# Expert loop of a mixture-of-experts decoder block: the down product one block further behind, waits at matmuls with fixed addresses, four buffers of turned rows

## What is computed

```python
probs = jax.nn.softmax(x @ gate_w, axis=-1)
w, sel = jax.lax.top_k(probs, K)                  # K = 8 of E = 32
w = w / jnp.sum(w, axis=-1, keepdims=True)
...
xg = x_pad[t_slot].reshape(E, C, H)               # the queue of each expert
g = jnp.einsum('ech,ehi->eci', xg, w_gate)        # H = 256, i = 96
u = jnp.einsum('ech,ehi->eci', xg, w_up)
y = jnp.einsum('eci,eih->ech', jax.nn.silu(g) * u, w_down).reshape(E * C, H)
out = jnp.zeros((T + 1, H), x.dtype).at[t_slot].add(w_slot[:, None] * y)
```

## Time and profile before

| | us |
|---|---|
| median of 3 runs | 625.38 |
| lowest and highest run | 624.90, 626.18 |
| span of the profiled execution | 719.4 |
| attention stages in it, up to | 350 |
| PE's expert loop in it | 389.4 to 658.5 |
| PE busy in the span | 563.9 (78%) |
| ACT, DVE, POOL busy | 330.1, 368.4, 390.5 |

### The profile page before, as it was taken

The page is one execution under the profiler, slowest core; times in us unless marked ns, Lnnn a source line. Parts: engine busy times, 40 slices in busy tenths (PEclk is TensorE's granted clock), DMA queues, the critical chain, the costliest instruction groups (busy, mean ns, idle before and its releaser), DMA issues.

```text
span 719.4 us, 17476 instructions
## 1 busy us (share of the span) xinstructions
PE 563.9 (78%) x5097; PEld 414.4 (58%) x5098; DVE 368.4 (51%) x1527; ACT 330.1 (46%) x1204; POOL 390.5 (54%) x599
## 2 busy tenths in 40 slices
PE   3768787888878888888306889988998888985995
PEld 2445454544555554444105777777777776774884
DVE  1537566666677566666402444444444444443453
ACT  2445555455455455456003555555555554553012
POOL 5443445545544455545551666766666666665432
PEclk9789999999999899999556999999999999998899
DMA  9999996111111111112285554555555454554994
GB/s 206 277 275 365 342 339 231 69 59 73 68 50 64 55 73 73 65 66 74 99 308 182 155 165 150 160 156 167 152 164 159 143 157 142 164 160 148 425 418 145
DMA packets 83069, 121.31 MB, mean 169 GB/s; under 512 B 13779, under 2 KB 72669, under 8 KB 80992
## 3 DMA queue, kind: packets, MB, share of 16 engines
q1 hardware_dynamic: 64128, 78.46, 36.3%
q0 software_dynamic: 14016, 38.44, 14.7%
q10 hardware_dynamic: 4896, 4.03, 1.7%
HBM read 56.07 MB, written 69.01 MB: 174 GB/s over the span
## 4 chain that ended last, share of the span: by engine, by line
PE 54%; issue 12%; ACT 12%; DVE 9%; DMA 6%; ACTq 3%; POOL 2%; SPq 1%; another core or an unknown queue 0%; DVEq 0%; POOLq 0%
PE bank L793 14%; PE bank L809 9%; ACT pr L870 7%; PE bank L611 5%; PE bank L785 5%; PE bank L601 4%; PE bank L803 3%; PE bank L661 3%; DMA out<-fin 3%; PE bank L744 2%; DMA wall<-results 2%; DVE nmax L1024 2%; PE bank L619 2%; ACTq L296 1%; DVE tg L1218 1%
## 5 line engine op out<-in xcount | busy, mean ns | idle before, releaser
L556 POOL DMA_INDIRECT results<-ys,wcol x152 | 150.1, 988 | 25.8 <-POOL pscrap L545 22.0
L530 POOL DMA_INDIRECT queues<-x,xidx x128 | 129.1, 1009 | 36.9 <-issue 36.5
L793 PE MATMUL bank<-wall,xtT 128*128 x616 | 127.1, 330 | 0.7 <-issue 0.7
L870 ACT ACTIVATE pr<-bank,nmax 128x128 f32<-128x128 f32 x256 | 90.9, 370 | 29.1 <-DVE nmax L1024 29.1
L1218 DVE SCALAR_TENSOR_TENSOR tg<-th,bank 128x96 f32<-128x96 f32 x154 | 39.1, 254 | 125.3 <-ACT th L957 96.9
L793 PEld LDWEIGHTS bank<-wall,xtT 128*128 128x128 f32 x616 | 98.4, 194 | 1.4 <-issue 1.3
L963 ACT ACTIVATE ys<-bank,wcol 128x256 f32<-128x256 f32 x152 | 71.9, 473 | 54.6 <-PE bank L809 36.6
L809 PE MATMUL bank<-wall,hT 96*128 x304 | 94.5, 392 | 0.0
L785 PE MATMUL bank<-ident,xt 128*128 128x128 f32 x310 | 63.3, 286 | 35.4 <-DMA xt<-queues 24.1
L785 PEld LDWEIGHTS bank<-ident,xt 128*128 128x128 f32 x310 | 59.0, 197 | 49.9 <-DMA xt<-queues 25.1
L876 ACT COPY prT<-bank 128x512 f32<-128x512 f32 x64 | 38.5, 601 | 88.9 <-PE bank L611 86.2
(11 more groups left out here) (178 smaller groups left out, 947.2 us busy)
## 6 DMA issues: line engine op xcount, KB each, us to landing
xt<-queues SPq DMA_DIRECT2D x162, 160.0 KB
results<-zeros SPq DMA_DIRECT2D x16, 1024.0 KB
wall<-results SPq DMA_DIRECT2D x16, 1024.0 KB, 12.7
queues<-zeros SPq DMA_DIRECT2D x32, 160.0 KB, 4.9
wall<-in_L_ffn_w_gate SPq DMA_DIRECT2D x4, 768.0 KB
wall<-in_L_ffn_w_up SPq DMA_DIRECT2D x4, 768.0 KB
wall<-in_L_ffn_w_down SPq DMA_DIRECT2D x4, 768.0 KB
results<-ys,wcol POOLq DMA_INDIRECT x152
```

Of the source, the lines that this page charges most:

```text
L530: pool.indirect_dma_start(xg, bass.IndirectOffsetOnAxis(ap=xidx[:, par, k:k + 1], axis=0), x2[:, par, :], None, bounds_check=last_row, oob ...
L556: pool.indirect_dma_start(yr, bass.IndirectOffsetOnAxis(ap=wcol[:, u, 1:2], axis=0), ys[:, u, :], None, bounds_check=last_y, oob_is_err=Fa ...
L793: ins = pe.matmul(bank[2 + u % 2][:, 0:2 * INTER].rearrange("p (g i) -> p g i", g=2), xtT[:, u % 2, kk, :], wall[:, bass.ds(e, GU)].rearrange(
L870: ins = act.activation(pr[:, g % 2, q, :], pS[g % 2][:, q * P:(q + 1) * P], ACT.Exp, bias=nmax[:, 4 * g + q:4 * g + q + 1], accum_out=den[ ...
```

## The change

The loop's body for block t becomes, on PE, `block_T(t + 4)`, `gu(t + 3)`, `turn_h(t + 2)`, `down(t)`, and on ACT and DVE correspondingly; `weights` stays at t + 2. So the down product comes two blocks behind the turn of its rows, not one, and `hT` has four buffers. The wait for `dveF["hT"]` ahead of `down` is gone, and the semaphore with it: on DVE the copy of block t's `hT` stands ahead of the gate of block t + 2, for which PE's `turn_h(t + 2)`, ahead of `down(t)`, waits. The wait for `actF["xT"]` moves from `gu` to the second transpose of `block_T`, whose address is fixed. Three registers are carried from round to round, and the lead-in has one block more.

```diff
--- before.py
+++ after.py
@@ -30,6 +30,7 @@
 LEAD = UN - 2
+DEEP = 3
 IDLE = 2 * UN + 2
...
         hg = sb("hg", [P, 2, INTER])
-        hT = sb("hT", [INTER, 2, P])
+        hT = sb("hT", [INTER, 4, P])
         wcol = sb("wcol", [P, UN, 2], I32)
...
         actF = {n: sem(f"actF_{n}") for n in ("xT", "th", "y")}
-        dveF = {n: sem(f"dveF_{n}") for n in ("w", "tg", "hg", "hT")}
+        dveF = {n: sem(f"dveF_{n}") for n in ("w", "tg", "hg")}
         drained = sem("drained")
...
@@ -779,16 +780,14 @@
                 s = u % UN
 
                 pe.wait_ge(xt_in[s], 16 * (j + (u // UN + 1)))
-                if isinstance(t, int) and t >= 2:
-                    pe.wait_ge(actF["xT"], t - 1)
-                for kk in range(2):
-                    ins = pe.transpose(bank[u % 2][:, kk * P:(kk + 1) * P],
-                                       xt[:, s, kk:D:2], ident[:, :])
-                ins.then_inc(peF["xT"], 1)
+                pe.transpose(bank[u % 2][:, 0:P], xt[:, s, 0:D:2], ident[:, :])
+
+                if there(t - 1):
+                    pe.wait_ge(actF["xT"], t)
+                pe.transpose(bank[u % 2][:, P:2 * P], xt[:, s, 1:D:2], ident[:, :]).then_inc(peF["xT"], 1)
 
             def gu(t, u, e):
 
-                pe.wait_ge(actF["xT"], t + 1)
                 for kk in range(2):
                     ins = pe.matmul(bank[2 + u % 2][:, 0:2 * INTER].rearrange("p (g i) -> p g i", g=2),
                                     xtT[:, u % 2, kk, :],
@@ -805,28 +804,32 @@
 
             def down(t, u, e):
 
-                pe.wait_ge(dveF["hT"], t + 1)
-                pe.matmul(bank[6 + u % 2][:, 0:D], hT[:, u % 2, :], wall[0:INTER, bass.ds(e, WX)][:, GU:WX],
+                pe.matmul(bank[6 + u % 2][:, 0:D], hT[:, u % 4, :], wall[0:INTER, bass.ds(e, WX)][:, GU:WX],
                           start=True, stop=True).then_inc(peF["y"], 1)
             for t in range(3):
                 block_T(t, t, 0)
-            last_two = [nc.alloc_register(ET.PE, f"last_two{u}") for u in range(2)]
-            carried = [bass.RuntimeValue.of_register_unchecked(r).with_bounds(min_val=0, max_val=(NE - 1) * WX) for r in last_two]
-            for t, e in zip((0, 1), neighbours(ET.PE, tab_g[0:1, LEAD:UN], (NE - 1) * WX)):
-                pe.reg_mov(last_two[t], e)
-                gu(t, t, e)
+            last = [nc.alloc_register(ET.PE, f"last{u}") for u in range(DEEP)]
+            carried = [bass.RuntimeValue.of_register_unchecked(r).with_bounds(min_val=0, max_val=(NE - 1) * WX) for r in last]
+            first = neighbours(ET.PE, tab_g[0:1, LEAD:LEAD + DEEP], (NE - 1) * WX)
+            for t in range(DEEP):
+                pe.reg_mov(last[t], first[t])
+            gu(0, 0, first[0])
+            block_T(3, 3, 0)
+            gu(1, 1, first[1])
             turn_h(0, 0)
+            gu(2, 2, first[2])
+            turn_h(1, 1)
             with pe.Fori(0, rounds) as j:
-                e = neighbours(ET.PE, tab_g[0:1, bass.ds(j * UN + UN, UN)], (NE - 1) * WX)
+                e = neighbours(ET.PE, tab_g[0:1, bass.ds(j * UN + LEAD + DEEP, UN)], (NE - 1) * WX)
                 for u in range(UN):
                     t = j * UN + u
-                    block_T(t + 3, u + 3, j)
-                    gu(t + 2, u, e[u])
-                    turn_h(t + 1, u + 1)
-                    down(t, u, e[u - 2] if u >= 2 else carried[u])
-                for u in range(2):
-                    pe.reg_mov(last_two[u], e[UN - 2 + u])
+                    block_T(t + 4, u + 4, j)
+                    gu(t + 3, u + 3, e[u])
+                    turn_h(t + 2, u + 2)
+                    down(t, u, e[u - DEEP] if u >= DEEP else carried[u])
+                for u in range(DEEP):
+                    pe.reg_mov(last[u], e[UN - DEEP + u])
...
@@ -968,13 +971,15 @@
                 act.copy(spare[0:1, k:k + 1], tab_n[0:1, 0:1]).then_inc(actF["y"], 1)
             for t in range(3):
                 block_T(t, t)
-            for t in range(2):
-                tanh(t, t)
+            tanh(0, 0)
+            block_T(3, 3)
+            tanh(1, 1)
+            tanh(2, 2)
             with act.Fori(0, rounds) as j:
                 for u in range(UN):
                     t = j * UN + u
-                    block_T(t + 3, u + 3)
-                    tanh(t + 2, u)
+                    block_T(t + 4, u + 4)
+                    tanh(t + 3, u + 3)
                     y(t, u)
...
@@ -1224,20 +1229,22 @@
             def h_T(t, u):
 
                 dve.wait_ge(peF["hT"], t + 1)
-                dve.tensor_copy(hT[:, u % 2, :], bank[4 + u % 2][0:INTER, 0:P]).then_inc(dveF["hT"], 1)
+                dve.tensor_copy(hT[:, u % 4, :], bank[4 + u % 2][0:INTER, 0:P])
 
             for t, column in zip((0, 1), neighbours(ET.DVE, tab_w[0:1, 0:UN], D + NE - 1)[LEAD:]):
                 weights(t, t, 0, column)
             for t in range(2):
                 gate(t, t)
             h_T(0, 0)
+            gate(2, 2)
+            h_T(1, 1)
             with dve.Fori(0, rounds) as j:
                 columns = neighbours(ET.DVE, tab_w[0:1, bass.ds(j * UN + UN, UN)], D + NE - 1)
                 for u in range(UN):
                     t = j * UN + u
                     weights(t + 2, u + 2, j, columns[u])
-                    gate(t + 2, u)
-                    h_T(t + 1, u + 1)
+                    gate(t + 3, u + 3)
+                    h_T(t + 2, u + 2)
```

## The result

The changed kernel takes 657.38 us (median of 4 runs, 656.0 to 658.51) against 625.78 us (4 runs, 624.9 to 626.59) for the kernel before: 1.051 times, 95% interval 1.049 to 1.0531. That is 31.6 us slower. The forecast was 624.3 us with a range up to 628.3, so it was wrong by far more than its range.

The account below looks back on a forecast made before the run. The prediction took PE's own pace, 11.4 us a round, plus 0.77 us around each turn as the bound. From 625.38 us, -3.4 at the turns and +2.3 in the lead-in gave 624.3 us, range 616.0 to 628.3.

Parts of the forecast that it names:

- The table load: At the round's turn on PE's sequencer: 557 to 809 ns, not hidden, some 0.5 us of the gap stay.
- The choice on late signals: Loop: L803's 34 waits for hg (27.9 us in 17 rounds) are a cost of being profiled, absent from the runs.
- Rival 1: Loop: the late hg signals are real, so L809's waits go in the runs too: 618.2 us, at most 614; chance 0.15.
- the forecast span of 712 us: Profiled execution: L809's idle 0.16 us behind each of some 38 late hg falls away, -6.1 us more.
- -3.4 us at the turn: Round's turn: without the wait on hT, address work starts at hg's end, 0.19 us earlier at 18 turns.
- The wait that was removed: Down product's wait on hT at the turn: its removal was to bring the 0.19 us.
- +2.3 us of lead-in: Ahead of the loop: one more block and a later first load delay its start by 2.3 us, bounds +1.5 to +3.1.
- The other zeros: Loop: the moved xtT wait, POOL, the block loads and the extra register move were each to cost nothing.
- Rival 2: Round's turn: the sequencer passes a waiting matmul, so the whole turn is hidden, -13.9 us: 613.8 us; chance 0.07.
- Rival 3: Round's first block: DVE's late gate takes back the turn's gain, lead-in stays: 627.7 to 628.5 us; chance 0.17.
- the forecast of -1.1 us: Whole kernel: -3.4 us at the turns and +2.3 us in the lead-in.

Follow-up runs that it names:

- b0_before: The kernel before, unchanged, run again for a second profiled execution: 624.12 us, span 622.5 us.
- a1_aligned: The changed kernel with PE's table of gate offsets written earlier, so each round's load begins at entry 8j + 8: 627.43 us, 1.0035.
- d_mid2: The changed kernel with both table loads, PE's and DVE's, moved to mid-round, from entry 8j + 12: 615.71 us, 0.984.
- a2_wait_back: The changed kernel with loads at 8j + 8 and the wait on hT put back at the down product: 627.48 us, 1.0036.
- b_w1: The kernel before with DVE's table one entry later and its loads at 8j + 9, PE's loads untouched: 640.97 us, 1.0247.
- c_mid2: The kernel before with both table loads, PE's and DVE's, moved to mid-round, from entry 8j + 12: 617.21 us, 0.9859.
- b_shift1: The kernel before with PE's table one entry later and its loads at 8j + 9: 657.36 us, 1.0538.
- b_shift2: The kernel before with PE's table two entries later and its loads at 8j + 10, one run: 657.66 us.

## Why the prediction was wrong, step by step

**The table load: the step that failed.** The prediction took the load's 557 to 809 ns as given, and said of its place at the turn that it "isn't hidden". Both are true of the kernel before. What it didn't price is that the change moves the load's start from 8j + 8 to 8j + 9, though the index stands in the diff. It costs, in the traces, 2.223 - 0.668 us (the means over the turns) x 18 turns = 28.0 us, and 1.948 - 0.601 = 1.35 us for the load of the first round: 29.3 us. Nothing covers the added part, for PE has some 0.35 us of queued matmuls left when the load begins. No bound was set on a load from another start, as there was no row for it in the trace; that absence should have widened the range upward.

**The rest of the 31.6 us.** From the traces of before (span 622.5) and after (655.4): the first transposes of the loop start at 334.31 instead of 328.93 us, 5.4 us later: 1.35 of it is the first slow load, 0.95 that the first block was turned later (323.66 for 322.71), and about 3.1 the longer lead-in. From there to the last turn it is 248.05 instead of 220.43 us: 27.6. Together 33.0 us, and the spans differ by 32.9. Of the 27.6 us, 25.9 are 18 rounds at 13.68 instead of 12.245 us; the other 1.8 are one slow stretch in the first round, behind the slow load (see the last section). A round is only 1.44 us longer, though its load is 1.555: the change gained 0.12 us at each turn, of which the next paragraphs tell.

**The choice on late signals** gave the right number for a wrong reason. They are not in the runs, as the forecast said, and the turn was worth 0.66 + 0.11 us, the round 12.2 us: 12.245 in b0_before. But they aren't the cost of being profiled, for which the prediction took them: the spans of b0_before and of the changed kernel are 1.6 and 2.4 us below their runs. Rival 1 falls with them, and so does the forecast span of 712 us.

**-3.4 us at the turn: the register work moved as forecast, the gain didn't come.** Over the 18 turns of b0_before (medians) the register instruction of L809 starts 0.04 us behind the end of the hT copy and 0.16 us ahead of L803's matmul; in a1_aligned L807's starts 0.05 us behind the end of hg and 0.35 us ahead of L802's matmul. That is 0.19 us earlier, just as the prediction had it. Two things then took it back. The third register move is in one instruction with the others, as forecast, but that instruction takes 103 ns in place of 47, and "nothing" should have been 0.056 us. And the load, which begins 0.115 us earlier, takes 0.752 us in the mean in place of 0.668. With the first block, 0.03 us longer, the round of a1_aligned is 12.236 us long, that of b0_before 12.246: 0.2 us gained in all. The wait of the round's first transposes for issue, forecast to shrink from 16.8 to 13.5 us in 17 rounds, is 16.1 there, for 16.6 in b0_before. Why the load is longer there is open. It isn't simply that matmuls run beside it, for in d_mid2 it lies wholly beside them and takes 0.596 us.

**The wait that was removed** gained nothing by itself (a2_wait_back). The prediction put the 0.19 us down to it. With the wait put back the register work still starts 0.05 us behind hg, so the 0.19 us comes with the extra block of distance.

**+2.3 us of lead-in: within its bounds, at the upper one.** a1_aligned is 2.5 us slower than before. In its trace the loop starts 3.0 us later, 3.1 us counted from the first transposes. Step by step: L792 starts 3.15 us behind the first transposes where L793 started 2.35 us behind them, +0.8 as forecast. The copy of block 2 ends at 327.85, near where the forecast had it (its 388.5 is 327.6 on this trace's time by the first transposes, 328.0 by the loop's start in b0_before). The second group of L792 then ends 1.83 us behind it, where 0.65 to 1.3 was allowed; from there on all is as forecast. (Two roundings of the prediction are 0.1 us off and bear on nothing: its 385.5 should be 385.4, the 623.4 of its bounds 623.5.) The group ran at half clock until 329.5:

```profile
328.19 1.49 PE L792 MATMUL bank<-wall,xtT 128*128 x4
```

```profile
325.00:329.50 4.50, 3.63 (x12) 2.83 (x12) 0.51 (x2) 0.53 (x2) 0.00 (x0) 0.50 0.45 140
```

**The other zeros held.** The moved wait on xtT shows nowhere in the loop's waits, POOL and the block loads cap nothing, and blocks stay 1.42 us apart. Rival 2 is refuted: with a fast load the turn is as long as before, and the register work still comes behind hg. Rival 3 gave 627.7 us for "no gain at the turn, lead-in paid", and a1_aligned measured 627.43. But its mechanism (a late gate on DVE) isn't what did it, since no wait of L802 for hg is in its waits list. (The prediction also names the place of such a wait twice, as the second L803 of a round and as one in its first block; b_w1 shows it in the second.)

With the load's start kept, then, the forecast of -1.1 us stands against +2.5 measured. That would still have been a miss of the sign, mostly by the turn, where 0.2 us of the 3.4 were gained; the changed start made it +31.6.

## What to carry to other kernels

When a change moves the index of a load into registers, look at where it begins: here a shift of one entry was worth 29 us, more than all the waits that the change was about, and writing the table from another entry gave it back. An instruction that stays in the diff with another operand is not the same instruction; if the trace has no row for the new operand, its price is unknown and belongs in the range. And where the sequencer's own work sets a gap, moving that work to a place where the engine has matmuls queued pays (8 to 10 us here), if the same work of the partner engine moves with it.

## What the runs showed of the hardware

- **A load of 8 registers from a table had two prices, by its start.** From a multiple of four 4-byte entries (8j + 8, 8j + 12, 8j + 16) PE's loads in the loop took 0.59 to 0.85 us, DVE's 0.6 (but for one of 0.80 and one of 1.09); from 8j + 9 or 8j + 10 PE's took 1.95 to 2.38 us, from 8j + 9 DVE's 1.85 to 2.33. Loads of two entries took 0.55 to 0.57 us from entries 6, 7, 8 and 10 alike. These prices hold in the loop and just ahead of it. Some 20 us earlier DVE's first load of 8, from entry 0, took 2.09 us in b0_before, and 6.54 in b_w1, where it is from entry 1. What makes loads longer there, no run shows:

```profile
L288 DVEq TENSOR_LOAD <-tab_w x1: 2089/2089/2089, 302.6 to 302.6; - x1
```

```profile
L288 DVEq TENSOR_LOAD <-tab_w x1: 6540/6540/6540, 303.0 to 303.0; - x1
```

- **Register work stays behind a matmul that is held.** At all 18 turns of a1_aligned the address work of L807 starts 0.05 us behind the end of hg, for which L802 ahead of it waits, and in b0_before L809's starts 0.04 us behind the end of hT, for which it waits itself.
- **Register moves in one instruction.** On PE one move took 37 ns, two took 47 or 65, three 80 to 125, by kernel and place.
- **Little is queued when the load begins.** PE then has 0.24 us of matmuls left at the turn of the kernel before, 0.35 us at that of the changed one, 0.64 us in mid-round in c_mid2 and 0.83 us in d_mid2 (medians, to the end of the last one). In d_mid2 the load of 0.6 us leaves no wait on the matmul row, and the round is 0.23 us above PE's own pace; a load of 2.2 us would be covered in none.
- **The clock fell to half (1.2 of 2.4 GHz) behind a few of the long gaps.** In the changed kernel PE was idle for 1.85 us from 332.46, behind the slow load of the first round. The granted clock was full from 332.4 to 335.8, and half from there to 339.2. The second block took 2.78 us and the third 1.66 in place of 1.42, 1.6 us in all. The windows (columns as in the earlier trace rows):

```profile
332.50:335.70 3.20, 1.39 (x9) 1.34 (x10) 0.88 (x4) 0.60 (x3) 0.00 (x0) 1.00 0.07 10
335.80:339.10 3.30, 3.30 (x12) 2.82 (x12) 1.54 (x8) 1.23 (x4) 1.25 (x2) 0.50 0.38 121
339.30:345.00 5.70, 5.70 (x38) 5.37 (x37) 2.76 (x14) 3.81 (x13) 4.43 (x8) 1.00 0.52 158
```

In the loop b_shift1 had two such stretches, from 346.6 and 568.4, and b_shift2 one, from 499.9, each in the round behind a gap of 2.15 to 2.24 us. Their first blocks were slow as well (2.84 us; 2.84 and 2.72), since the half clock of the lead-in lasted until 332.9 and 336.1 there. The kernels with fast loads on PE, b_w1 among them, had none in the loop. Most gaps of 2.2 us brought none either, and which do, the runs don't say.
